# Attention on one Trainium2 core: weighing the values for two key chunks at a time

## The chip, the cores and the metric

The kernel runs on one core of one Trainium2 chip. The metric is the device time of one execution in microseconds (us). A core has the engines PE (TensorE, matmul; its weight loads are listed as PEld), DVE (VectorE), ACT (ScalarE), POOL (GpSimd) and the DMA queue of SP (SyncE). They run side by side and wait for each other through semaphores.

## The reference

The program is one transformer layer: a modulated layer norm, causal attention, and a routed feed-forward part. Only the attention is touched by the change. Its core, for 8 sequences of 1024 tokens, 16 heads of 32 columns:

```python
q, k, v = proj(w_q, b_q), proj(w_k, b_k), proj(w_v, b_v)          # 8 x 16 x 1024 x 32 each
scores = jnp.einsum('bhqd,bhkd->bhqk', q, k) / np.sqrt(D_K)
scores = jnp.where(causal, scores, -jnp.inf)
attn = jax.nn.softmax(scores, axis=-1)
out = jnp.einsum('bhqk,bhkd->bqhd', attn, v).reshape(B, S, D_MODEL)
```

## The kernel before, in words

The program has five stages: modulation, the projections to q, k and v, attention, output projection with routing and shared part, and the experts. Attention works on 32 groups (8 sequences times 4 groups of 4 heads), one after the other, as a pipeline over groups: while the probabilities of one group (`prev` in the code) are computed, the row maxima of the next group (`cur`) are found.

The probabilities of a group are cut into 12 chunks. A chunk is one block of 128 keys against one half (512) of the queries, for all four heads; the list `chunks` gives (half, key block) of each. Because attention is causal, a chunk has 512, 384, 256 or 128 columns. In this text a *place* c is the part of a group's step in which chunk c is computed (chunks count from 0), c = 0 to 11. At a place PE issues, for each of the four heads h:

- one matmul that gives the scaled scores of chunk c minus the row maximum (L871, tile `ps_p`, three banks), and a masking matmul where the chunk lies on the diagonal (L874). ACT makes exponentials of it (L718) in a tile `pt`. The matmul waits until the exponential three matmuls earlier is done, since it takes over its bank;
- `TILES[4c+h]` score tiles of the next group (function `scores`, L815, tile `ps_s`, four banks). DVE takes the row maxima of each (L751, L757). A score tile waits until the maxima four tiles earlier are done. There are 48 score tiles in a group, spread over places 0 to 9.

After the four heads of place c, PE *weighs* the chunk before, c-1: `weigh` (L825) multiplies exponentials by values and adds up in the bank `ps_o`. Each head gives only 32 output rows, so four such matmuls stand beside each other in the array (128*32 in the profile, "column-tiled"); a chunk takes 8 instructions in the trace. The chunks 10 and 11 of a group are weighed at place 11 and at place 0 of the next group.

The sums of the exponentials are made in two steps. POOL *joins* tiles of exponentials (`join`, L677: one tile added into another in place, as `INTO` says), which works when the chunk was weighed, and PE multiplies what is left by ones (`total`, L842, column-tiled as well): one tile for the first query half at place 8, two tiles for the second half, of the group before, at place 3 (`TOTAL_AT`). A total takes one of the four `ps_s` banks, at the position that `BEFORE` works out from `TOTAL_AT`; ACT copies it out (L703) and the bank is free again.

At place 10 (`TURN`) PE transposes the row maxima (L850), DVE negates them and splits them in a high and a low part (L769, L771), and SP writes both as two more rows of the queries in SBUF (L628). The first matmul of place 0 of the next group waits for them (`m_in`). The order of everything is written out by hand; there is no scheduler.

Of the kernel before, what the change touches and what calls it, by code (L numbers as in the profile page):

```python
# [20 lines left out]
GH = P // HD  # L21
# [19 lines left out]
CREDIT = 16  # L41
# [414 lines left out]
def stage_attention(nc, qk_dram, v_dram, o_dram, inv_dram):  # L456
# [14 lines left out]
    with ExitStack() as ctx:  # L471
# [49 lines left out]
        NPROB = NC * GH  # L521


        INTO = {1: 0, 2: 0, 3: 0, 5: 4, 7: 6, 8: 4, 9: 4, 10: 6, 11: 6}
        JOINS = sorted(INTO)
        NJ = len(JOINS)
        HEADS = [[0], [4, 6]]
        TOTAL_AT = (8, 3)
        LATER = (3, 11)


        TILES = [3, 0, 1, 1, 1, 2, 1, 1, 2, 1, 1, 0, 2, 1, 1, 1, 2, 0, 1, 1,
# [115 lines left out]
        def _(pool):  # L648
# [21 lines left out]
            def join(group, c):  # L670

                col = span(c)
                into = tile(INTO[c])[:, :, col:UNIT]
                pool.wait_ge(pv_done, CREDIT + NC * group.g + c + 1)
                pool.sem_inc(mark, 1)
                pool.wait_ge(add_done, CREDIT + NJ * group.g + JOINS.index(c))
                pool.tensor_tensor(into, into, tile(c)[:, :, col:UNIT], ALU.add).then_inc(add_done, 1)  # L677
# [11 lines left out]
        def _(act):  # L689
# [15 lines left out]
            def step(cur, prev):  # L705
                if not prev:
                    return
                for c in range(NC):
                    col = span(c)
                    user, back = user_before(c)  # L710
                    for h in range(GH):
                        n = c * GH + h
                        if h == 0 and user in INTO:
                            act.wait_ge(add_done, CREDIT + NJ * (prev.g - back) + JOINS.index(user) + 1)
                        if h == 0 and user not in INTO:
                            act.wait_ge(sum_done, CREDIT + QH * (prev.g - back) + chunks[user][0] + 1)
                        act.wait_ge(p_done, CREDIT + NPROB * prev.g + n + 1)
                        act.activation(tile(c)[:, h, col:UNIT], ps_p[n % NP][:, col:UNIT], ACT.Exp,  # L718
                                       scale=float(HD) ** -0.5).then_inc(exp_done, 1)
                        group = prev if c >= 2 else older(prev)  # L720
                        if h == 0 and (c - 2) % NC in ENDS and group:
                            take(group, (c - 2) % NC)
                        if h == 0 and c == TOTAL_AT[0] + 1:
                            take_total(prev, 0)
                        if h == 0 and c == TOTAL_AT[1] + 1 and older(prev):
                            take_total(older(prev), 1)
# [70 lines left out]
        def _(pe):  # L797
# [20 lines left out]
            def weigh(group, c):  # L818
                qh, kt = chunks[c]
                col = span(c)  # L820
                if kt == 0:
                    pe.wait_ge(o_free, CREDIT + QH * group.g + qh)
                pe.wait_ge(exp_done, CREDIT + NPROB * group.g + (c + 1) * GH)
                for h in range(GH):
                    last = pe.matmul(ps_o[h * HD:(h + 1) * HD, col:UNIT], vs[group.slot][:, kt, h * HD:(h + 1) * HD],  # L825
                                     tile(c)[:, h, col:UNIT], start=kt == 0, stop=c in ENDS)
                last.then_inc(pv_done, 1)
# [24 lines left out]
            def step(cur, prev):  # L852
# [6 lines left out]
                for c, (qh, kt) in enumerate(chunks):  # L859
# [17 lines left out]
                            scores(cur, prev, share[n], share[n + 1])  # L877
                    group = prev if c else older(prev)
                    if group:
                        weigh(group, (c - 1) % NC)  # L880
                    if c == TOTAL_AT[0]:
                        total(prev, 0, cur)
                    if c == TOTAL_AT[1] and older(prev):
# [1 line left out]

            steps(step)(pe)
            end = Group(GROUPS - 1, (GROUPS - 1) % SLOT, None)
            weigh(end, NC - 1)
            total(end, 1, None, alone=(NC - 2, NC - 1))

# [941 lines left out]
```

## Time and profile before

| what | value |
|---|---|
| median of 3 runs | 3338.03 us (3325.95 to 3339.06) |
| the profiled execution | 3321.04 us, its span 3319.3 us |
| attention | from 695 to 1870 us of the span, 31 turns of about 36.7 us and the two ends |
| PE in a group of 36.70 us | 36.33 us busy |
| DVE, ACT, POOL in the same group | 26.19, 22.63, 27.99 us busy |

A line of the timeline has the start in us from the start of the span, the time, the engine, the line of the kernel, the operation, the tiles written and read, the shape, and how many instructions were merged. In square brackets stands how long the engine was idle before it and what released it. The time of a matmul is modelled and overlaps with the next; how long a piece of work really takes on PE is therefore read from start to start. Idle time on PEld in front of a column-tiled load is put down to whatever semaphore that instruction also waits for, even where that had been given long before.

### The profile page before, as it was taken

To read this page: it belongs to the slowest core of one execution; us is meant where nothing else is said; L and a number is where in the kernel's file an instruction comes from. 1 tells how busy PE (TensorE), PEld (TensorE's weight loads), DVE (VectorE), ACT (ScalarE), POOL (GpSimd) and SP (SyncE) were. 2 spreads that over 40 slices of the span, in tenths; PEclk is the share of its full clock that TensorE was granted. 3 is DMA by queue.
4 is the path that set the end of the run, shared out by engine and by line. 5 is a ranking of instruction groups with operands and counts; after the bars stand their busy time and mean duration, and the time that the engine had idled before them with its cause. 6 is when DMAs were issued, how large, how long until landed. Compare 5 with 4: busy or idle time off the path is not lost. (4 is left out here: it accounts for less than half of the span.)

```text
span 3319.3 us, 52119 instructions
## 1 busy us (share of the span) xinstructions
PE 3023.0 (91%) x16704; PEld 2188.1 (66%) x16704; DVE 2144.3 (65%) x5331; ACT 1384.5 (42%) x2755; POOL 1888.6 (57%) x1107
## 2 busy tenths in 40 slices
PE   3999999789999999999999669999999999966997
PEld 0888888655556556555656258777777777745776
DVE  3545555377767776777677257778777777735674
ACT  1212222136666666566666432332332233214674
POOL 2332332237777777777777525565664765653664
PEclk7999999979999999999999789999999999977998
DMA  8556555555445544554453323323323223107996
GB/s 163 172 173 209 180 199 174 160 123 129 111 105 127 131 105 105 129 129 104 111 129 79 100 81 111 102 67 98 114 67 98 89 92 92 60 13 214 236 241 132
DMA packets 297669, 419.49 MB, mean 126 GB/s; under 512 B 64776, under 2 KB 148744, under 8 KB 297495
## 3 DMA queue, kind: packets, MB, share of 16 engines
q1 hardware_dynamic: 274974, 383.70, 41.9%
q0 software_dynamic: 22528, 33.72, 5.2%
q8 instruction: 86, 1.41, 0.2%
q14 instruction: 81, 0.66, 0.1%
HBM read 262.85 MB, written 153.01 MB: 125 GB/s over the span
## 5 line engine op out<-in xcount | busy, mean ns | idle before, releaser
L677 POOL TENSOR_TENSOR att_pt<-att_pt 128x2048 f32<-128x2048 f32 (+3 forms) x286 | 892.2, 3120 | 319.2 <-PE att_ps_o L825 306.0
L718 ACT ACTIVATE att_pt<-att_ps_p 128x512 f32<-128x512 f32 (+3 forms) x1536 | 679.7, 496 | 491.8 <-PE att_ps_p L874 291.9
L751 DVE CUSTOM_DVE_ANT_0 att_ps_s<-att_ps_s,att_causal 128x512 f32<-128x512 f32 (+3 forms) x1024 | 492.8, 505 | 152.4 <-PE att_ps_s L815 148.8
L871 PE MATMUL att_ps_p<-att_qs,att_ks 98*128 98x512 f32 (+3 forms) x1536 | 555.3, 386 | 6.7 <-DMA att_qs<-att_m_lo 3.2
L815 PE MATMUL att_ps_s<-att_ks,att_qs 96*128 96x512 f32 (+3 forms) x1536 | 487.9, 375 | 22.7 <-DMA att_ks<-qk_parts 22.0
L871 PEld LDWEIGHTS att_ps_p<-att_qs,att_ks 98*128 98x128 f32 x1536 | 288.9, 190 | 280.3 <-ACT att_pt L718 172.9
L757 DVE TENSOR_REDUCE att_lower<-att_ps_s 128x1 f32<-128x512 f32 x512 | 352.0, 688 | 178.7 <-PE att_ps_s L815 176.9
L1140 POOL DMA_INDIRECT slot_info<-ffn_info,ffn_slot x256 | 272.8, 1065 | 123.9 <-issue 77.6
L815 PEld LDWEIGHTS att_ps_s<-att_ks,att_qs 96*128 96x128 f32 x1536 | 278.1, 194 | 76.0 <-issue 22.4
L825 PE MATMUL att_ps_o<-att_pt,att_vs 128*32 128x512 f32 (+3 forms) x3072 | 328.0, 499 | 0.0
L311 POOL TENSOR_TENSOR qkv_x<-qkv_x,qkv_mod 128x512 f32<-128x512 f32 x64 | 91.1, 1424 | 363.6 <-DVE qkv_x L378 363.6
L1104 POOL TENSOR_TENSOR ffn_h<-ffn_h,ffn_mod 128x512 f32<-128x512 f32 x48 | 75.1, 1564 | 301.9 <-DVE ffn_h L1258 301.9
L874 PE MATMUL att_ps_p<-att_mask_k,att_ident_r 128*128 128x128 f32 x1024 | 240.1, 238 | 0.0
L1422 PE MATMUL ffn_ps_m<-ffn_dn_hi,ffn_a_hi 128*128 128x512 f32 x512 | 210.1, 410 | 9.1 <-DVE ffn_a_lo L1383 6.1
L400 DVE SCALAR_TENSOR_TENSOR qkv_out_lo<-qkv_ps_m,qkv_bqk,qkv_out_hi 128x512 fp32r<-128x512 f32 x128 | 93.4, 746 | 178.3 <-ACT qkv_out_hi L355 178.3
L1422 PE MATMUL ffn_ps_m<-ffn_dn_hi,ffn_a_lo 128*128 128x512 f32 x512 | 204.7, 400 | 2.4 <-issue 2.4
L1422 PE MATMUL ffn_ps_m<-ffn_dn_lo,ffn_a_hi 128*128 128x512 f32 x512 | 205.2, 401 | 1.3 <-issue 1.2
L1422 PE MATMUL ffn_ps_m<-ffn_hT_hi,ffn_up_hi 128*128 128x512 f32 x512 | 202.3, 395 | 3.3 <-issue 3.2
L1422 PE MATMUL ffn_ps_m<-ffn_hT_lo,ffn_up_hi 128*128 128x512 f32 x512 | 200.4, 391 | 3.6 <-issue 3.6
L1422 PE MATMUL ffn_ps_m<-ffn_hT_hi,ffn_up_lo 128*128 128x512 f32 x512 | 200.6, 392 | 2.7 <-issue 2.6
L443 PE MATMUL qkv_ps_m<-qkv_hT_hi,qkv_w_hi 128*128 128x512 f32 x512 | 200.5, 392 | 1.5 <-DVE qkv_hT_lo L383 1.5
L443 PE MATMUL qkv_ps_m<-qkv_hT_lo,qkv_w_hi 128*128 128x512 f32 x512 | 200.2, 391 | 0.0
(263 smaller groups left out, 6229.3 us busy)
## 6 DMA issues: line engine op xcount, KB each, us to landing
att_qs<-qk_parts SPq DMA_DIRECT2D x96, 512.0 KB, 6.8
att_ks<-qk_parts SPq DMA_DIRECT2D x96, 512.0 KB, 13.2
qk_parts<-qkv_out_hi SPq DMA_DIRECT2D x128, 256.0 KB, 2.6
qk_parts<-qkv_out_lo SPq DMA_DIRECT2D x128, 256.0 KB, 2.9
qkv_x<-x SPq DMA_DIRECT2D x16, 1024.0 KB, 5.5
v_rows<-qkv_out_v SPq DMA_DIRECT2D x64, 256.0 KB, 2.3
att_vs<-v_rows SPq DMA_DIRECT2D x32, 512.0 KB, 16.0
o_parts<-att_o SPq DMA_DIRECT2D x64, 256.0 KB, 6.6
```

The source lines that it names most:

```text
L400: dve.scalar_tensor_tensor(out_lo[n % RING][:, :], ps_m[n % BANKS][:, :], bqk_sb[:, n:n + 1], raw(out_hi[n % RING][:, :]), op0=ALU.add, op ...
L443: last = pe.matmul(ps_m[n % BANKS][:, :], w_part[:, k, (n % NG) * P:(n % NG + 1) * P], h_part[:, k, :], start=k == 0 and a + c == 0, stop= ...
L677: pool.tensor_tensor(into, into, tile(c)[:, :, col:UNIT], ALU.add).then_inc(add_done, 1)
L718: act.activation(tile(c)[:, h, col:UNIT], ps_p[n % NP][:, col:UNIT], ACT.Exp, scale=float(HD) ** -0.5).then_inc(exp_done, 1)
L751: dve.tensor_tensor_reduce(bank, bank, causal[:, UNIT - (c1 - c0):UNIT], scale=1.0, scalar=MASKED, op0=ALU.add, op1=ALU.max, accum_out=row ...
L757: dve.reduce_max(lower[:, low:low + 1], bank, axis=AX.X).then_inc(max_done, 1)
L815: pe.matmul(ps_s[at % NS][:, 0:c1 - c0], qs[cur.slot][0:STACK, h, t * P:(t + 1) * P], ks[cur.slot][0:STACK, h, c0:c1], start=True, stop=Tr ...
L825: last = pe.matmul(ps_o[h * HD:(h + 1) * HD, col:UNIT], vs[group.slot][:, kt, h * HD:(h + 1) * HD], tile(c)[:, h, col:UNIT], start=kt == 0 ...
L871: last = pe.matmul(ps_p[n % NP][:, col:UNIT], ks[prev.slot][:, h, kt * P:(kt + 1) * P], qs[prev.slot][:, h, q0:(qh + 1) * UNIT], start=Tru ...
L874: last = pe.matmul(ps_p[n % NP][:, col:col + P], ident_r[:, :], mask_k[:, :], start=False, stop=True)
L1140: pool.indirect_dma_start(info_dram[:, :], bass.IndirectOffsetOnAxis(slot[half][:, j:j + 1].bitcast(U32), 0), info[half][:, j, :], None, b ...
L1422: last = pe.matmul(bank, a[m], c[n], start=i + j == 0, stop=i + 1 == len(pairs) and j == 2)
```

## The change

Three things are changed. A table `RUNS` now says at which place which chunks are weighed: chunks 0 and 1 at place 2, 2 and 3 at place 4, 4 and 5 at place 6, 6 and 7 at place 8, chunk 8 at place 9, chunk 9 at place 10, and 10 and 11 together at place 0 of the next group. Places 1, 3, 5, 7 and 11 weigh nothing. The total of the second half moves from place 3 to place 2 (`TOTAL_AT`), where it stands right behind the weighing of chunk 1 and not of chunk 2, and the bank that it takes moves with it. A join now waits for the exponentials of the chunk that it reads and for the weighing of the tile that it writes, and no longer for the weighing of the chunk that it reads; that wait has gone to ACT, which now asks for it before it overwrites the tile. Chunk 7 is joined into the tile of chunk 4 instead of that of chunk 6, which is weighed only at place 8.

```diff
-        INTO = {1: 0, 2: 0, 3: 0, 5: 4, 7: 6, 8: 4, 9: 4, 10: 6, 11: 6}
+        INTO = {1: 0, 2: 0, 3: 0, 5: 4, 7: 4, 8: 4, 9: 4, 10: 6, 11: 6}
-        TOTAL_AT = (8, 3)
+        TOTAL_AT = (8, 2)
+        RUNS = {0: (10, 11), 2: (0, 1), 4: (2, 3), 6: (4, 5), 8: (6, 7), 9: (8,), 10: (9,)}
@@ join
-                pool.wait_ge(pv_done, CREDIT + NC * group.g + c + 1)
+                pool.wait_ge(exp_done, CREDIT + NPROB * group.g + (c + 1) * GH)
+                pool.sem_inc(mark, 1)
+                pool.wait_ge(pv_done, CREDIT + NC * group.g + INTO[c] + 1)
@@ scalar step
                             act.wait_ge(add_done, CREDIT + NJ * (prev.g - back) + JOINS.index(user) + 1)
+                            act.wait_ge(pv_done, CREDIT + NC * (prev.g - back) + user + 1)
@@ tensor step
                     group = prev if c else older(prev)
                     if group:
-                        weigh(group, (c - 1) % NC)
+                        for done in RUNS.get(c, ()):
+                            weigh(group, done)
@@ tensor, behind the last group
+            weigh(end, NC - 2)
             weigh(end, NC - 1)
```

The first place to look at is the end of one group and the start of the next, on PE. Before, from the last head of place 11 on; pt5 holds chunk 10 and pt6 chunk 11:

```order
L874 MATMUL att_ps_p2<-att_mask_k,att_ident_r 128x128
L825 MATMUL att_ps_o<-att_pt5,att_vs0 32x256 [waits att_exp]
L825 MATMUL att_ps_o<-att_pt5,att_vs0 32x256 x3
L871 MATMUL att_ps_p0<-att_qs1,att_ks1 128x512 [waits att_v_in1,att_exp,att_m_in1,att_q_in2]
```

In the changed kernel, from the same instruction to the end of place 0, on PE (lines are 4 higher there):

```order
L878 MATMUL att_ps_p2<-att_mask_k,att_ident_r 128x128
L875 MATMUL att_ps_p0<-att_qs1,att_ks1 128x512 [waits att_v_in1,att_exp,att_m_in1,att_q_in2]
L878 MATMUL att_ps_p0<-att_mask_k,att_ident_r 128x128
L819 MATMUL att_ps_s0<-att_ks2,att_qs2 128x512 [waits att_mlo]
...
L819 MATMUL att_ps_s0<-att_ks2,att_qs2 128x512 [waits att_max]
L829 MATMUL att_ps_o<-att_pt5,att_vs0 32x256 [waits att_exp]
L829 MATMUL att_ps_o<-att_pt5,att_vs0 32x256 x3
L829 MATMUL att_ps_o<-att_pt6,att_vs0 32x128 [waits att_exp]
L829 MATMUL att_ps_o<-att_pt6,att_vs0 32x128 x3
```

The weighing of chunk 10 has moved behind the work of place 0, to that of chunk 11; the matmul that waits for the rows of the maxima (`att_m_in1`) now follows place 11 directly.

The second is places 2 and 3, on PE, the weighings and the total alone. Before, pt0, pt3 and pt4 hold chunks 0, 1 and 2, pt1 and pt2 what is to be summed of the group before, and between the weighings stand the matmuls of a place each:

```order
L825 MATMUL att_ps_o<-att_pt0,att_vs1 32x512 [waits att_exp,att_o_free]
...
L825 MATMUL att_ps_o<-att_pt3,att_vs1 32x384 [waits att_exp]
...
L825 MATMUL att_ps_o<-att_pt4,att_vs1 32x256 [waits att_exp]
L825 MATMUL att_ps_o<-att_pt4,att_vs1 32x256 x3
L842 MATMUL att_ps_s3<-att_pt1,att_ones 32x512 [waits att_add,att_max]
L842 MATMUL att_ps_s3<-att_pt1,att_ones 32x512 x3
L842 MATMUL att_ps_s3<-att_pt2,att_ones 32x512 x4
```

In the changed kernel, the end of place 2 on PE:

```order
L829 MATMUL att_ps_o<-att_pt0,att_vs1 32x512 [waits att_exp,att_o_free]
L829 MATMUL att_ps_o<-att_pt0,att_vs1 32x512 x3
L829 MATMUL att_ps_o<-att_pt3,att_vs1 32x384 [waits att_exp]
L829 MATMUL att_ps_o<-att_pt3,att_vs1 32x384 x3
L846 MATMUL att_ps_s2<-att_pt1,att_ones 32x512 [waits att_add,att_max]
L846 MATMUL att_ps_s2<-att_pt1,att_ones 32x512 x3
L846 MATMUL att_ps_s2<-att_pt2,att_ones 32x512 x4
```

Chunk 0, chunk 1 and the total are now one stretch of column-tiled matmuls, in which no score tile is issued; chunk 2 has gone to the end of place 4, and the total takes bank 2 instead of bank 3.

## Rows read from the trace of the kernel before

**Rows 1.** Busy time by engine in one group, turn to turn; of each engine, busy us and instructions.

```profile
core 0: us, PE busy (x) PEld busy (x) DVE busy (x) ACT busy (x) POOL busy (x), PEclk, DMA share, GB/s
1208.80:1245.50 36.70, 36.33 (x249) 21.90 (x249) 26.19 (x85) 22.63 (x53) 27.99 (x10) 1.00 0.53 117
```

**Rows 2.** Timeline of PE, turn and end of place 11.

```profile
1208.84 0.27 PE L850 MATMUL att_ps_s<-att_ident,att_rowmax 128*32 128x128 f32 x1 [0.30 <-DVE att_rowmax L764]
...
1212.06 0.33 PE L871 MATMUL att_ps_p<-att_qs,att_ks 98*128 98x128 f32 x1
...
1212.43 0.64 PE L825 MATMUL att_ps_o<-att_pt,att_vs 128*32 128x256 f32 x8
1213.00 0.50 PE L871 MATMUL att_ps_p<-att_qs,att_ks 98*128 98x512 f32 x1
```

**Rows 3.** Timeline of PE, places 7 to 9 of that group.

```profile
1237.74 1.06 PE L825 MATMUL att_ps_o<-att_pt,att_vs 128*32 128x512 f32 x8
1238.73 0.50 PE L871 MATMUL att_ps_p<-att_qs,att_ks 98*128 98x512 f32 x1
1239.08 0.23 PE L815 MATMUL att_ps_s<-att_ks,att_qs 96*128 96x128 f32 x1
...
1239.66 0.40 PE L871 MATMUL att_ps_p<-att_qs,att_ks 98*128 98x512 f32 x1
1239.90 0.40 PE L815 MATMUL att_ps_s<-att_ks,att_qs 96*128 96x512 f32 x1
...
1240.37 0.51 PE L815 MATMUL att_ps_s<-att_ks,att_qs 96*128 96x128 f32 x2
1240.81 0.85 PE L825 MATMUL att_ps_o<-att_pt,att_vs 128*32 128x384 f32 x8
1241.48 1.04 PE L842 MATMUL att_ps_s<-att_pt,att_ones 128*32 128x512 f32 x8
```

**Rows 4.** Timeline of PE, end of place 2: a weighing of 384 columns alone.

```profile
1221.07 0.85 PE L825 MATMUL att_ps_o<-att_pt,att_vs 128*32 128x384 f32 x8
1221.86 0.33 PE L871 MATMUL att_ps_p<-att_qs,att_ks 98*128 98x128 f32 x1
```

**Rows 5.** Timeline of ACT, the exponentials of place 11.

```profile
1211.73 1.08 ACT L718 ACTIVATE att_pt<-att_ps_p 128x128 f32<-128x128 f32 x4 [1.04 <-PE att_ps_p L874]
```

**Rows 6.** Who waited for whom in attention (us in total, times, longest).

```profile
PEld att_ps_s L815 <- ACT att_total L703: 9.0, 30, 0.3
```

**Rows 7.** Timeline of POOL: joins.

```profile
1205.18 16.61 POOL L677 TENSOR_TENSOR att_pt<-att_pt 128x1536 f32<-128x1536 f32 x5 [1.61 <-PE att_ps_o L825]
```

**Rows 8.** Timeline of PE: the total at place 3.

```profile
1224.29 1.90 PE L842 MATMUL att_ps_s<-att_pt,att_ones 128*32 128x512 f32 x16
```

**Rows 9.** Timeline of DVE: idle behind the turn and the total; then three tiles.

```profile
1213.88 0.69 DVE L757 TENSOR_REDUCE att_lower<-att_ps_s 128x1 f32<-128x512 f32 x1 [3.93 <-PE att_ps_s L815]
...
1226.99 0.57 DVE L751 CUSTOM_DVE_ANT_0 att_ps_s<-att_ps_s,att_causal 128x384 f32<-128x384 f32 x1 [1.68 <-PE att_ps_s L815]
...
1229.74 0.69 DVE L757 TENSOR_REDUCE att_lower<-att_ps_s 128x1 f32<-128x512 f32 x1
...
1231.20 0.69 DVE L757 TENSOR_REDUCE att_lower<-att_ps_s 128x1 f32<-128x512 f32 x1
```

**Rows 10.** Timeline of PE: places 5 and 6, each with the weighing behind it.

```profile
1228.58 0.50 PE L871 MATMUL att_ps_p<-att_qs,att_ks 98*128 98x512 f32 x1
...
1230.80 1.07 PE L825 MATMUL att_ps_o<-att_pt,att_vs 128*32 128x512 f32 x8
1231.79 0.50 PE L871 MATMUL att_ps_p<-att_qs,att_ks 98*128 98x512 f32 x1
...
1234.41 1.06 PE L825 MATMUL att_ps_o<-att_pt,att_vs 128*32 128x512 f32 x8
```

**Rows 11.** Timeline of SP, the second row of the maxima.

```profile
1210.04 0.59 SPq L628 DMA_DIRECT2D att_qs<-att_m_lo  x1
```

**Rows 12.** The tile m_lo in attention: issue to landing.

```profile
DMA to landing us min/median/max: 2.1/2.1/3.0
```

## The prediction

> **What bounds the kernel now.** I read the busy time by engine over one group first, then the timelines of PE, ACT, DVE and POOL over the same group, and last the list of waits. In a group of 36.70 us PE is busy for 36.33, and no other engine for more than 27.99 [rows 1]. The clock column there is 1.00, so PE runs at its upper level throughout. PE's only idle time of note is 0.30 us at the turn [rows 2]. So attention lasts as long as PE's instruction stream, and what counts is how long each piece really holds PE, read from start to start.
>
> There the stream has a price that the busy figure hides: a column-tiled stretch costs more than its work. Three parts of it can be read.
> - In front: two score tiles start at 1240.37; one of 512 columns takes 0.24 (1239.66 to 1239.90), one of 128 a quarter, 0.06, so the weighing could start at 1240.67; it starts at 1240.81. That is 0.14 us [rows 3].
> - At its end: a weighing of 384 columns with a full-width matmul behind it takes 0.79 us [rows 4], with another column-tiled stretch behind it 0.67 us (1240.81 to 1241.48) [rows 3]. That is 0.12 us.
> - Behind: the first full-width matmul holds PE for 0.35 us (1238.73 to 1239.08), a later one of the same size for 0.24 [rows 3]. That is 0.11 us.
>
> Together 0.37 us for each weighing that stands alone. A group has twelve such stretches now (the totals stand behind weighings) and seven after the change.
>
> **The change part by part.**
>
> Chunks 0, 2, 4 and 6 join the next chunk's weighing (four stretches fewer): 4 x 0.37 = 1.48 us. The multiplications themselves stay. Nothing lies beside this time, since PE is the engine that is full; what takes it back is whoever is late next, below.
>
> Chunk 10 goes from place 11 to place 0. Before, place 0 starts at 1213.00 [rows 2]. Now its first matmul directly follows place 11, but must have the exponential three matmuls back, the second of place 11. Those four start at 1211.73 and take 1.08, so the second ends at 1212.27 [rows 5]; the handover is 0.06 (the first ends at 1212.00, and the matmul that waits for it starts at 1212.06 [rows 2]). So place 0 starts at 1212.33, 0.67 earlier, and without the 0.11 behind a tiled stretch: 0.78. The work comes back at the end of place 0: 256 columns, about 0.42 (from 512 alone, 0.99, to 384 alone, 0.79, it is 0.20 for each 128 [rows 3, 4]; from 0.67 for 384 inside a stretch it is 0.22). Net 0.36 us; one wait, on ACT, is all that this edit uncovers.
>
> The second total moves from place 3 to place 2. It stands behind a weighing before and after, so it changes no stretch. But the bank that it takes is now asked for by a tile late in place 3, where ACT has only exponentials of 128 columns in front of the copy; before, PE waited for the copy in 30 groups, 9.0 us [rows 6], 0.30 each. I count 0.25 back; the ends are 0 and 0.30.
>
> The joins wait for exponentials. POOL is not what PE waits for as long as the second total finds its joins done. Before: five joins from 1205.18 to 1221.79 [rows 7], the total at 1224.29 [rows 8], 2.5 us to spare. Counted from the start of place 0 (1213.00), the joins start at -7.8. Now the 1.61 us of idle in front of them goes [rows 7] (chunk 7 no longer waits to be weighed), the join in front of that can start one weighing earlier (1.0, the first half of a pair being enough), and the shorter group costs 1.5: -8.9, and with 16.6 of work they end at 7.7. The total comes at 8.9: place 3 began at 1221.86, which is 8.86 [rows 4], plus 0.42 for chunk 10 and less 0.37 for a stretch. 1.2 us to spare: cost 0. Were that gone, each us of lateness would be a us of PE at place 2. The wait moved to ACT costs nothing either: the tile that it writes at place 8 was weighed at place 2, and the latest such pair is chunk 9, weighed at place 10 and overwritten at place 2 of the next group. Behind a late ACT stands PE, which needs its banks.
>
> What is late next is DVE, and that is the one new cost. Today every place has a weighing behind it, in which DVE catches up. Now two places follow each other, and PE may be four tiles ahead at most. Places 5 and 6 are the worst, with 12 tiles in `TILES`. DVE needs 1.46 us for three (1229.74 to 1231.20 [rows 9]), 0.49 each, 5.84 for twelve. PE took 2.22 and 2.62 for the two places, up to each weighing [rows 10]; less the 0.14 and 0.11 that go, 4.59. When PE issues the twelfth tile, eight of the twelve and about one and a half left over must be done: 9.5 x 0.49 = 4.6, and some 0.4 from the first tile to DVE's start, 5.0. PE is held for about 0.45 us. Ends: 0, if DVE is level at the start, and 5.84 - 4.59 = 1.25, if DVE paces both places. The pairs 1 and 2 (9 tiles), 3 and 4 (9) and 7 and 8 (10) I put at 0.10 together.
>
> Sum for a group: 1.48 + 0.36 + 0.25 - 0.45 - 0.10 = 1.54 us. There are 31 turns: 47.7 us. The last group, where no score tiles stand between and PE often waits for ACT, I put at 1.3, a little less than a turn: 49 us.
>
> The profiled execution took 3321.0 us (span 3319.3), and 3321.0 - 49 is 3272. The three timed runs are 3326 to 3339; with the profiled one the mean is 3331. I set the gain against that: 3282 us.
>
> At one point the Trainium skill speaks against this. Rows 3 let a column-tiled matmul follow another nearly free: 384 columns take 0.67 for some 0.60 to 0.64 of work. The Trainium skill ("TensorE: Matmul & The Clock Gate", Part 3: Packing small matmuls — row/col tiling) says that a weight load overlaps with matmuls in flight only if it goes to other rows of the array; column tiles share all rows. By that rule each of the five joints in the pairs would show its loads again, and I would put them at the 0.14 that the front of a stretch costs, in place of 0.03: 0.55 us a group, 17 us in all, and 3299 us. The trace had this joint 0.67 us long, which speaks for the row.
>
> **The rivals.**
>
> Half the gain (3299 to 3310 us). The mechanism is right, but more is given back: DVE holds PE by 1.25 us instead of 0.45, which leaves 0.74 us x 31 = 23 us, 3308. Or the rows of the maxima come late: the second is issued at 1210.04 [rows 11] and lands after 2.1 us, 1212.14, only 0.19 before place 0 can now start; the longest took 3.0 [rows 12], which would be 0.7 us late, and for all groups 22 us. For it: margins shrink from 0.86 to 0.19 us. Against it: minimum and median are both 2.1. The rule above belongs here too.
>
> No gain (3315 to 3347, the change doesn't do what it says). The 0.37 us might not be a price of changing width but of the wait for exponentials in which each weighing stands, in which case fewer stretches leave it where it is. Against it: the last scores matmul in front of each weighing has already waited for a later exponential than the weighing needs, and the 0.11 behind the stretch has nothing to wait for.
>
> Slower (3353 us). DVE becomes the bound. It works 26.2 us of a group and is idle for 10.5 [rows 1]: 3.93 at the turn and 1.68 behind the total, the rest smaller [rows 9]. After the change the tiled stretches last about 3.5 us at place 2 (0.99 + 0.67 + 1.9 [rows 3, 8]), 2.6 at place 8 and 1.9 at place 6. If DVE enters each with four tiles (1.95 us) it idles 2.0, 1.1 and 0.4 with the refill, and 3.8 around the turn, 7.3 in all: 33.5 us, below the 35.2 of PE. With two tiles only, as when PE's own waits keep it from running ahead, it loses 0.97 more at each of four stretches: 37.4 us a group, 0.7 over today, +22 us. It decides from 2.4 tiles down, (36.7 - 33.5) / 4 = 0.8 us less than four. Against it: today PE keeps DVE fed up to each weighing, and it will issue faster.
>
> **How the numbers follow.** What can be told from no change is about 0.5%, 17 us on 3331. Forecast 0.60, with its own range 3265 to 3298 (2.1 us a group with DVE never in the way; 1.05 with 0.95 of holding). Half the gain 0.24, no gain 0.10, slower 0.06. Faster by over 0.5%: 0.84; within: 0.10; slower: 0.06. For 8 in 10 I take 3260 to 3316, which holds the half gain and leaves out the last two cases.
>
> **What would show it.** Right: turns 35.1 to 35.3 us apart; a pair of 512 and 384 columns that takes about 1.65 us to the total; place 0 about 3.5 us behind the turn instead of 4.16; waits of PE for DVE's maxima, today hardly there, at places 5 and 6, with some 0.5 us a group; longer single idle times of DVE at place 3 (above 2 us) and none between 1 and 2; POOL idle before fewer joins. Wrong: a second chunk in a pair that takes 0.14 us more than its columns (the skill's rule); a wait for m_lo at every place 0; turns at 36 us with DVE without gaps (DVE the bound); or turns at 36.7 with idle time in front of the pairs (the price was a wait).

## The result

The changed kernel takes 3623.72 us (median of 4 runs, 3597.67 to 3641.42) against 3331.99 us before. The ratio is 1.0858, with a 95% interval of 1.0819 to 1.0898: about 290 us slower, where 49 us faster was forecast. Between the first and the last turn lie 31 turns: before, they take 36.79 us each on average (nearly all 36.70), now 46.04. 31 x 9.25 = 287 us, so attention holds the whole loss. In the experiments below, where some runs of a kernel lie more than 1.5% above its fastest (e5, e6, e10), the ratio is taken from the others and so is smaller than the quotient of the medians.

The page of the changed kernel, parts 1 and 2 (engine, busy us; below, slices of the span in tenths):

```profile
span 3633.0 us, 52405 instructions
...
PE 3248.5 (89%) x16704; PEld 2376.2 (65%) x16704; DVE 2213.6 (61%) x5331; ACT 1399.9 (39%) x2755; POOL 1886.7 (52%) x1107
...
PEclk7999999677788787877778777999999999997998
```

The last row is what to look at first. In the attention, where the old page has a 9 in every slice that lies wholly in it, the clock that was granted to TensorE is 7 or 8 tenths. No engine was given more work: the page of before has the same counts of instructions (16704 matmuls, 5331 on DVE, 1107 on POOL).

One group of the changed kernel, then the stretches before and behind its turn (columns as in [rows 1]; the clock stands behind the busy times):

```profile
core 0: us, PE busy (x) PEld busy (x) DVE busy (x) ACT busy (x) POOL busy (x), PEclk, DMA share, GB/s
1234.60:1237.30 2.70, 0.06 (x4) 0.00 (x0) 2.59 (x1) 0.45 (x1) 2.62 (x2) 1.00 0.00 0
1237.30:1242.60 5.30, 5.27 (x26) 3.48 (x26) 0.77 (x3) 2.14 (x7) 5.22 (x2) 0.55 0.04 8
1242.60:1252.80 10.20, 10.20 (x44) 7.95 (x45) 5.02 (x15) 4.94 (x11) 2.87 (x2) 0.50 0.27 69
```

PE stands still for 2.7 us with the clock still up; then the clock is at the lower of its two levels, 0.50, which is 1.2 GHz, through places 10 and 11 and well into the next group. DVE is busy through the idle time with a single instruction. The timelines of PE and DVE there:

```profile
1233.59 1.06 PE L829 MATMUL att_ps_o<-att_pt,att_vs 128*32 128x512 f32 x8
1237.33 0.27 PE L854 MATMUL att_ps_s<-att_ident,att_rowmax 128*32 128x128 f32 x1 [2.68 <-DVE att_rowmax L768]
```

```profile
1234.11 0.14 DVE L755 DVE_READ_ACCUMULATOR2_ANT att_rowmax<- 128x1 f32 x1
1234.40 2.79 DVE L768 TENSOR_TENSOR att_rowmax<-att_rowmax,att_lower 128x16 f32<-128x16 f32 x1
1237.64 0.28 DVE L773 TENSOR_SCALAR att_m_hi<-att_ps_s 32x128 fp32r<-32x128 f32 x1 [0.45 <-PE att_ps_s L854]
```

The idle time answers to the 0.30 us at the turn in [rows 2]. What made it is the last step of the row maxima, an elementwise maximum of 16 columns. It took 2.79 us. The same line over all groups (ns: least, median, longest), in the changed kernel and then before:

```profile
L768 DVE TENSOR_TENSOR att_rowmax<-att_rowmax,att_lower x32: 177/2786/2807, 687.1 to 2111.4; 128x16 f32<-128x16 f32 x32
```

```profile
L764 DVE TENSOR_TENSOR att_rowmax<-att_rowmax,att_lower x32: 175/415/420, 692.2 to 1832.5; 128x16 f32<-128x16 f32 x32
```

It needs 0.18 us. Even before it took 0.42 in 28 of 31 turns. The join tile around that time shows what it stood behind: the joins of POOL in flight from 1234 to 1238 in the changed kernel:

```profile
L680 POOL TENSOR_TENSOR att_pt<-att_pt x2: 4524/4530/4535, 1232.6 to 1237.2; 128x2048 f32<-128x2048 f32 x2
```

One join runs from 1232.6 for 4.53 us, to 1237.15; the next starts at 1237.2. DVE's instruction ends at 1237.19. Before, the join of 384 columns ran from 1205.18 to 1208.66 and DVE's instruction from 1208.28 to 1208.70: it stood behind the tail of a join then, too, for a quarter of a microsecond. The change moved the joins earlier ([rows 7]: five joins that began when chunk 7 was weighed), and so put a join of 512 columns over the turn.

So far this is read from two traces: a cause (DVE behind POOL), an idle time, a clock, and no proof that one makes the next.

### The profile page after: what moved, and what is told of

Its sections match the earlier page's. It is cut to its first block and busy times, and to the rows that moved or that the text cites. A ratio compares the mean times of both kernels' runs of the same rounds, so it can differ in the third digit from the quotient of the medians.

```text
span 3633.0 us, 52405 instructions
## 1 busy us (share of the span) xinstructions
PE 3248.5 (89%) x16704; PEld 2376.2 (65%) x16704; DVE 2213.6 (61%) x5331; ACT 1399.9 (39%) x2755; POOL 1886.7 (52%) x1107
## 5 line engine op out<-in xcount | busy, mean ns | idle before, releaser
L722 ACT ACTIVATE att_pt<-att_ps_p 128x512 f32<-128x512 f32 (+3 forms) x1536 | 694.2, 496 | 769.7 <-PE att_ps_p L878 635.4
L875 PE MATMUL att_ps_p<-att_qs,att_ks 98*128 98x512 f32 (+3 forms) x1536 | 641.4, 440 | 6.5 <-DMA att_qs<-att_m_lo 3.2
L819 PE MATMUL att_ps_s<-att_ks,att_qs 96*128 96x512 f32 (+3 forms) x1536 | 584.1, 435 | 23.3 <-DMA att_ks<-qk_parts 22.2
L875 PEld LDWEIGHTS att_ps_p<-att_qs,att_ks 98*128 98x128 f32 x1536 | 355.3, 233 | 198.1 <-issue 143.9
L819 PEld LDWEIGHTS att_ps_s<-att_ks,att_qs 96*128 96x128 f32 x1536 | 331.5, 228 | 99.8 <-issue 22.5
L829 PE MATMUL att_ps_o<-att_pt,att_vs 128*32 128x512 f32 (+3 forms) x3072 | 367.2, 598 | 0.0
L878 PE MATMUL att_ps_p<-att_mask_k,att_ident_r 128*128 128x128 f32 x1024 | 292.1, 286 | 0.0
L878 PEld LDWEIGHTS att_ps_p<-att_mask_k,att_ident_r 128*128 128x128 f32 x1024 | 266.4, 260 | 12.3
## 6 DMA issues: line engine op xcount, KB each, us to landing
att_ks<-qk_parts SPq DMA_DIRECT2D x96, 512.0 KB, 12.9
```

The lines of the kernel that those rows point to most:

```text
L819: pe.matmul(ps_s[at % NS][:, 0:c1 - c0], qs[cur.slot][0:STACK, h, t * P:(t + 1) * P], ks[cur.slot][0:STACK, h, c0:c1], start=True, stop=Tr ...
L875: last = pe.matmul(ps_p[n % NP][:, col:UNIT], ks[prev.slot][:, h, kt * P:(kt + 1) * P], qs[prev.slot][:, h, q0:(qh + 1) * UNIT], start=Tru ...
L878: last = pe.matmul(ps_p[n % NP][:, col:col + P], ident_r[:, :], mask_k[:, :], start=False, stop=True)
```

## Experiments

The theory: DVE's last maximum, with both inputs in SBUF, waits for the POOL instruction in flight; PE then idles at the turn; and this idle time brings the clock down for some 20 us of nearly every group. Rival A: the new order of the matmuls (nothing weighed at place 11, long column-tiled stretches) lowers the clock by itself. Rival B: DVE is late for lack of score tiles, and the wait only shows at this instruction.

The kernels of one series share a chip and the runs of the kernel before; these were 3327, 3244 and 3306 us for the three series, so ratios are what can be compared. "Turn" is the mean distance over 31 turns, from the first to the last, in the profiled execution; for e10 that was the longest of its runs (3582 us). "Clock" is the mean granted clock in attention, 1.00 being the upper level.

| kernel | ratio to before (95% interval) | turn, us | clock in attention |
|---|---|---|---|
| before | 1 | 36.79 | 1.00 |
| changed | 1.0858 (1.0819 to 1.0898) | 46.04 | 0.80 |
| e1 one input | 0.9936 (0.9913 to 0.9959) | 35.94 | 1.00 |
| e2 hold | 1.0009 (0.9985 to 1.0032) | 36.85 | 1.00 |
| e3 old joins | 1.0018 (0.9996 to 1.0040) | 36.74 | 1.00 |
| e4 fill | 1.0227 (1.0185 to 1.0269) | 38.67 | 1.00 |
| e5 before, DVE +2.4 | 1.0895 (1.0861 to 1.0929) | 46.28 | 0.85 |
| e6 before, DVE +1.2 | 1.0963 (1.0927 to 1.0999) | | |
| e7 joins alone | 1.0250 (1.0223 to 1.0278) | 39.61 | 0.95 |
| e8 before, one input | 0.9989 (0.9975 to 1.0003) | 36.62 | 1.00 |
| e9 e8 and DVE +1.2 | 1.0261 (1.0237 to 1.0285) | 39.38 | 0.95 |
| e10 e8 and DVE +2.4 | 1.0694 (1.0655 to 1.0733) | 45.77 | 0.82 |
| e11 e1 again | 0.9921 (0.9901 to 0.9941) | 35.95 | 1.00 |
| e12 e1, a tile moved | 0.9914 (0.9896 to 0.9933) | 36.07 | 1.00 |

### e1: the same maximum with one SBUF input

```diff
-        lower = s.sb("lower", [P, GH * LOW], FP32)
+        both = s.sb("both", [P, GH * LOW, 2], FP32)
@@ the two halves of a maximum go side by side into both
-                                                 accum_out=rowmax[:, h * KT + t:h * KT + t + 1]).then_inc(max_done, 1)
+                                                 accum_out=(both[:, h * LOW + t - LOW, 1:2] if t >= LOW else
+                                                            rowmax[:, h * KT + t:h * KT + t + 1])).then_inc(max_done, 1)
-                        dve.reduce_max(lower[:, low:low + 1], bank, axis=AX.X).then_inc(max_done, 1)
+                        dve.reduce_max(both[:, low, 0:1], bank, axis=AX.X).then_inc(max_done, 1)
@@ negate
-                dve.tensor_tensor(upper, upper, lower[:, :].rearrange("p (h t) -> p h t", t=LOW), ALU.max).then_inc(max_done, 1)
+                dve.reduce_max(upper, both[:, :, :].rearrange("p (h t) s -> p h t s", t=LOW), axis=AX.X).then_inc(max_done, 1)
```

> The changed kernel; only the last step of the row maxima on DVE is another instruction: the two halves of a maximum are written side by side in one tile and taken together by a reduction with one SBUF input, in place of a tensor_tensor with two. Theory (DVE's instruction with two SBUF inputs stands behind the POOL join in flight, PE idles 2.7 us at every turn, and its clock falls): the instruction takes about 0.2 us also while a join runs, the idle time of PE at the turn goes from 2.68 to 0.1 to 0.4 us, the granted clock of the attention stage from 0.80 to 0.99 or more, turns 35.1 to 35.3 us apart, 3275 to 3295 us. Rival A (the new order of the matmuls itself lowers the clock: nothing to weigh at place 11, longer column-tiled stretches): the idle time goes, but the clock stays near 0.8 and the time is 3520 to 3560 us. Rival B (DVE is behind for lack of tiles after the long stretches, and the wait only shows at that instruction): the wait moves to another line, over 3550 us.

Measured: 3306.47 us, ratio 0.9936, clock 1.00. From its timeline, all engines together around a turn:

```profile
1225.77 4.57 POOL L680 TENSOR_TENSOR att_pt<-att_pt 128x2048 f32<-128x2048 f32 x1
...
1226.75 1.06 PE L830 MATMUL att_ps_o<-att_pt,att_vs 128*32 128x512 f32 x8
...
1227.56 0.19 DVE L769 TENSOR_REDUCE att_rowmax<-att_both 128x16 f32<-128x32 f32 x1
...
1227.89 0.27 PE L855 MATMUL att_ps_s<-att_ident,att_rowmax 128*32 128x128 f32 x1
```

A join of 4.57 us is in the middle of its run, and DVE's step takes 0.19 us beside it. Nothing else was changed, and the joins are where the change put them. The 2.68 us are gone, the clock stays up, and what is left of the change is a small gain. Rivals A and B both asked for over 3500 us and fall. The operation was changed together with the number of its SBUF inputs, so this run alone doesn't say which of the two frees it. The time is 11 us above my range, the turns (35.94, for 35.1 to 35.3) 0.6 us above theirs; more on that below.

### e2: POOL holds one join until the turn is past

```diff
             def join(group, c):
 
+                if c == 8 and group.g + 1 < GROUPS:
+                    pool.wait_ge(max_done, CREDIT + NM * (group.g + 2))
+                    pool.sem_inc(mark, 1)
                 col = span(c)
```

> The changed kernel, and POOL does not start the join of chunk 8 before DVE's last maximum of the turn is done; instructions are the same, only that join starts later (about 2.2 us). Theory: the same instruction of DVE, now with no join in flight, takes 0.18 us instead of 2.79, the clock stays up, 3275 to 3300 us; POOL ends its joins 2.2 us later, which may cost a wait at the total of place 2 of up to 1 us a group (30 us at most). Rival A (the order of the matmuls lowers the clock): 3520 to 3560 us. Rival B: no change, about 3620.

Measured: 3333.60 us, ratio 1.0009, clock 1.00. The tensor_tensor with two inputs is back, and no join runs beside it; over all groups it takes

```profile
L771 DVE TENSOR_TENSOR att_rowmax<-att_rowmax,att_lower x32: 174/175/177, 687.9 to 1830.2; 128x16 f32<-128x16 f32 x32
```

So it is not the instruction alone but the join beside it. That no gain was left has its main reason in the waits of PE in attention (us in total, times, longest):

```profile
PE att_ps_s L849 <- POOL att_pt L683: 22.7, 29, 0.9
```

The total at place 2 now waits 0.8 to 0.9 us for the last join in nearly every group, since the join of chunk 8 began 2.3 us later than in e1. That leaves 1.3 to 1.4 us as what the joins had to spare, against the 1.2 worked out in the prediction. The time is 34 us above my range of 3275 to 3300, which did not include the wait (put at 30 us at most).

### e3: the old rule for the joins

```diff
-                pool.wait_ge(exp_done, CREDIT + NPROB * group.g + (c + 1) * GH)
-                pool.sem_inc(mark, 1)
-                pool.wait_ge(pv_done, CREDIT + NC * group.g + INTO[c] + 1)
+                pool.wait_ge(pv_done, CREDIT + NC * group.g + c + 1)
```

> The changed kernel with the rule for joins of before (a join waits until the chunk that it reads was weighed); pairs, total at place 2 and the tile that chunk 7 is joined into stay. Theory: chunk 7 is joined when it is weighed at place 8, as before, which puts the end of that join at DVE's last maximum as before (0.42 us), and the join of chunk 8 behind it; the clock stays up; turns 35.3 to 36 us (the last join may reach the total of place 2 late), 3280 to 3310 us. Rival A: 3520 to 3620 us, since the order of the matmuls is that of the changed kernel. Rival B: the same.

Measured: 3333.98 us, ratio 1.0018, clock 1.00. Over all groups:

```profile
L766 DVE TENSOR_TENSOR att_rowmax<-att_rowmax,att_lower x32: 176/417/421, 689.4 to 1828.0; 128x16 f32<-128x16 f32 x32
```

The step takes 0.42 us as before the change, because the join of chunk 7 again starts when the chunk is weighed and ends at DVE's step. So the pairs alone do no harm; it takes the joins' rule. How much of the harm that rule does by itself, e7 shows. The time is 24 us above my range: the late joins cost PE 12.9 us in 29 waits at the total of place 2.

### e4: PE is kept busy while DVE is blocked

```diff
             def turn(cur, prev):
                 if prev:
+                    n = TURN * GH
+                    pe.wait_ge(exp_done, CREDIT + NPROB * prev.g + n - NP + 1)
+                    for _ in range(10):
+                        pe.matmul(ps_p[n % NP][:, :], ks[prev.slot][:, 0, 0:P], qs[prev.slot][:, 0, 0:UNIT], start=True, stop=True)
```

> The changed kernel with ten more matmuls of full width (512 columns, 2.4 us at the upper clock) on PE just before the turn, into a bank that the next scores overwrite; DVE's instruction still stands behind the join. This parts idle time from clock: if the clock falls because PE stands idle, it now stays at 0.99 though the turn comes as late as before, and the time is 3331 - 48 + 31 x 2.5 = 3360 us (3345 to 3380). If the clock falls by anything else in the new order, it stays near 0.8 and the time is 3600 us or more.

Measured: 3408.66 us, ratio 1.0227. The timeline of PE around a turn, and of DVE; below, attention as a whole:

```profile
1266.59 1.06 PE L829 MATMUL att_ps_o<-att_pt,att_vs 128*32 128x512 f32 x8
1267.58 2.60 PE L855 MATMUL att_ps_p<-att_qs,att_ks 98*128 98x512 f32 x10
1270.40 0.27 PE L858 MATMUL att_ps_s<-att_ident,att_rowmax 128*32 128x128 f32 x1 [0.22 <-DVE att_rowmax L768]
```

```profile
1267.41 2.85 DVE L768 TENSOR_TENSOR att_rowmax<-att_rowmax,att_lower 128x16 f32<-128x16 f32 x1
```

```profile
720.00:1880.00 1160.00, 1146.32 (x7799) 734.59 (x7801) 845.40 (x2563) 677.52 (x1567) 845.12 (x272) 1.00 0.48 108
```

DVE is blocked for 2.85 us as in the changed kernel, the turn comes as late, but PE works through it, and the clock stays at 1.00. This is the run that parts the two costs. Against e1 the block costs 38.67 - 35.94 = 2.73 us a turn, 85 us in all. Against e4 the changed kernel, with the same block and PE idle in it, loses another 46.04 - 38.67 = 7.37 us a turn, 228 us: the clock. The time was 29 us above my range.

### e5 and e6: idle time in the old order, and a dose that was not one

```diff
                 dve.wait_ge(max_done, CREDIT + NM * cur.g + N1)
                 dve.sem_inc(mark, 1)
+                if prev:
+                    for k in range(4):
+                        dve.reduce_max(junk[:, k:k + 1], causal[:, :], axis=AX.X)
```

e6 has `range(2)`.

> The kernel before, with four useless reductions of 512 columns (0.60 us each, 2.4 us) on DVE in front of the last maximum of every turn: the order of the matmuls and the joins are those of before, only PE must idle at the turn as in the changed kernel. Theory (idle time of some 2.7 us at the turn is enough to lower the clock): the clock of attention falls to 0.8, turns 46 to 48 us apart, 3600 to 3660 us. Rival A (it takes the new order too, with nothing weighed at place 11): the clock stays at 1.00, turns 39.1 us, 3327 + 31 x 2.4 = 3400 us.

> The same with two reductions (1.2 us): a smaller idle time at the same place. If the clock depends on the length of the idle time: it stays up and the time is 3327 + 31 x 1.2 = 3364 us. If any wait of over 1 us there is enough: the clock falls in many groups and it is over 3500 us. I expect the first, without a number of the trace for where the limit lies.

Measured: 3535.72 us, ratio 1.0895, and 3561.28 us, ratio 1.0963 (the profiled execution of e6 took 3804 us, so that only its mechanism is read and no turn or clock stands in the table). The first ratio is as expected. The second is far from it: half the delay costs as much and a little more. The waits of PE (from 720 to 1840 us) and DVE's step in e6 say why:

```profile
PE att_ps_s L854 <- DVE att_rowmax L768: 102.6, 21, 4.9
```

```profile
L768 DVE TENSOR_TENSOR att_rowmax<-att_rowmax,att_lower x32: 174/3800/3805, 687.3 to 2358.0; 128x16 f32<-128x16 f32 x32
```

A delay of 1.2 us carried the step into the next join, the one of chunk 8, and there it stood for 3.8 us; with 2.4 us of delay it met the same join later and took 2.62, and PE idled for 4.9 us in both. The two kernels gave the same dose of idle time, so they show that the order of before loses its clock as well, but not how much idle time it takes. They also show how near the old kernel lay: 1.2 us later, and it is 9.6% slower. In e5 every turn has the same 4.89 us of idle time, and yet after the first few the distance from one to the next alternates between 42.7 and 49.4 us, and the stretches at the lower clock between 6.8 and 20.5 us: how long it stays down is not set by the idle time alone.

### e7: the rule for the joins alone

```diff
-        INTO = {1: 0, 2: 0, 3: 0, 5: 4, 7: 6, 8: 4, 9: 4, 10: 6, 11: 6}
+        INTO = {1: 0, 2: 0, 3: 0, 5: 4, 7: 4, 8: 4, 9: 4, 10: 6, 11: 6}
-                pool.wait_ge(pv_done, CREDIT + NC * group.g + c + 1)
+                pool.wait_ge(exp_done, CREDIT + NPROB * group.g + (c + 1) * GH)
+                pool.sem_inc(mark, 1)
+                pool.wait_ge(pv_done, CREDIT + NC * group.g + INTO[c] + 1)
@@ scalar step
+                            act.wait_ge(pv_done, CREDIT + NC * (prev.g - back) + user + 1)
```

> The kernel before with the new rule for joins alone (exponentials of the chunk read, weighing of the tile written, chunk 7 into the tile of chunk 4); weighings stay single, the total at place 3. Theory: the join of chunk 8 now starts about 1241.5 in the old trace's time, when its exponentials are done, and takes 4.6 us; DVE's last maximum, at 1245.0, stands behind it for about 1.1 us. PE idles some 1.2 us at the turn: 3327 + 31 x 1.0 = 3358 us if the clock stays, over 3500 us if it falls. Rival B (the stall needs the pairs): 3327 us, no change.

Measured: 3324.06 us against 3243.96, ratio 1.0250. DVE's step over all groups, then attention:

```profile
L767 DVE TENSOR_TENSOR att_rowmax<-att_rowmax,att_lower x32: 176/1482/1770, 688.0 to 1914.4; 128x16 f32<-128x16 f32 x32
```

```profile
720.00:1900.00 1180.00, 1135.47 (x7423) 682.76 (x7419) 814.11 (x2528) 680.21 (x1550) 834.73 (x269) 0.95 0.48 106
```

The step stands behind the join for 1.3 us, near the 1.1 expected. Most turns are 37.80 us apart, 1.1 above before; five of the 31 are between 45 and 50 us, those in which the clock fell. The expectation of 1.0 us a turn if the clock stays was right for 26 of them; it gave two cases, and what came lies between.

This also corrects what e3 alone would suggest. The joins' rule without the pairs costs 39.61 - 36.79 = 2.82 us a turn, the whole change 9.25. One turn of e7, POOL (the first of these joins is that of chunk 8), then DVE:

```profile
1201.64 13.03 POOL L679 TENSOR_TENSOR att_pt<-att_pt 128x2048 f32<-128x2048 f32 x4
```

```profile
1204.75 1.50 DVE L767 TENSOR_TENSOR att_rowmax<-att_rowmax,att_lower 128x16 f32<-128x16 f32 x1
```

DVE reaches its step 3.11 us after the join's start here and 1.78 us after it in the changed kernel (1234.40 against the join that begins at 1232.6). With the pairs the same join blocks 1.3 us longer, PE idles 2.68 us and not 1.37, and the clock falls at every turn and not at five.

### e8: the kernel before with one input

The edit is that of e1, on the kernel before.

> The kernel before with the reduction with one SBUF input in place of the last tensor_tensor of the maxima. Theory: even before, that instruction stood behind a join for 0.24 us (0.42 instead of 0.18 us, ending 0.04 us behind the join in nearly every group); 0.2 us x 31 = 6 to 8 us less, 3320 us. It also says how much of the gain of the changed kernel with the same edit is due to the pairs.

Measured: 3241.37 us against 3243.96, ratio 0.9989 with an interval to 1.0003: what the whole time can tell is no change, but the turns are 36.62 instead of 36.79 us apart (5 us in all), and the step takes 0.19 us. The change without that step, from e8 to e11 with the same maximum (on two chips, both at clock 1.00 in attention), is worth 36.62 - 35.95 = 0.67 us a turn on average, and in most turns 0.8.

### e9 and e10: the dose without the port

The two edits together: e8, and two or four useless reductions in front of the last step.

> The kernel before with the reduction with one SBUF input and two useless reductions on DVE (1.2 us) in front of it: the dose without the port. The runs with two and with four reductions both idled for 4.9 us at most, because the delayed tensor_tensor then stood behind the next join; here it can't. Theory: PE idles 1.2 us less the slack of 0.2 at the turn; if it is a matter of length, the clock stays up in most groups as in the joins-alone run (1.5 us there, 27 of 31 turns at full clock), turns 37.5 us, ratio 1.008 to 1.012. Rival A has nothing against this number: with the old order it expects no fall at any length.

> The same with four reductions (2.4 us), about the idle time of the changed kernel (2.68), in the old order of matmuls. Theory (idle time alone lowers the clock): the clock falls once in nearly every group, turns 45 to 48 us, ratio 1.08 to 1.10. Rival A (the new order is needed too): clock 1.00, turns 38.7 us, ratio 1.02.

Measured: 3392.77 and 3563.37 us against 3306.05, ratios 1.0261 and 1.0694. The step itself takes 0.18 us in every group of both now. (The expectation of e9 tells e7 a little wrong: PE idled for 1.37 us there, and 26 turns kept their clock, not 27.) The waits of PE and the clock in e9, then in e10:

```profile
PE att_ps_s L855 <- DVE att_rowmax L769: 37.4, 29, 1.6
```

```profile
720.00:1900.00 1180.00, 1139.12 (x7466) 685.35 (x7462) 816.79 (x2608) 684.41 (x1560) 838.47 (x271) 0.95 0.48 106
```

```profile
PE att_ps_s L855 <- DVE att_rowmax L769: 62.4, 25, 2.8
```

```profile
720.00:2100.00 1380.00, 1303.94 (x7484) 785.63 (x7487) 864.59 (x2677) 699.49 (x1564) 838.36 (x271) 0.82 0.41 91
```

In the old order of matmuls, with no join involved, idle time of 1.26 us (in 28 of the 31 turns; 1.61 at most) cost the clock in 4 of 31 groups, idle time of 2.45 us (in 26 turns; 2.80 at most) in 22 of them (turns over 45 us). So idle time at the turn is enough, and the longer it is the more often the clock falls: 4 of 31 at 1.26 us, 5 at 1.37 (e7), 22 at 2.45, all at 4.89 (e5). What picks the groups that lose it at one and the same length, no run shows. The ratio of e9 is 1.026 and not the 1.010 I had written: the four falls, of 12 us each, are 49 us that I had named in words and left out of the number. e10 is a little below its range (1.08 to 1.10), since nine groups kept their clock. Runs of e10 differ by 58 us; that the number of falls differs between them is likely, but only one was profiled. The changed kernel, with 2.7 us in all groups, lost its clock in every one. Whether the new order adds something between the 22 and the 31 was not tried: no run has 2.7 us of idle time in all groups without the pairs.

### e11 and e12: e1 again, and one tile moved

e11 is the kernel of e1 on another chip. e12:

```diff
-        TILES = [3, 0, 1, 1, 1, 2, 1, 1, 2, 1, 1, 0, 2, 1, 1, 1, 2, 0, 1, 1,
-                 2, 2, 1, 1, 1, 3, 0, 2, 3, 0, 0, 2, 1, 1, 1, 2, 1, 2, 0, 0] + 2 * GH * [0]
+        TILES = [3, 0, 1, 1, 1, 2, 1, 1, 2, 1, 1, 0, 2, 1, 1, 1, 2, 1, 1, 1,
+                 2, 2, 1, 1, 1, 2, 0, 2, 3, 0, 0, 2, 1, 1, 1, 2, 1, 2, 0, 0] + 2 * GH * [0]
```

> The changed kernel with the one-input reduction once more, beside a kernel before on this chip: ratio 0.991 to 0.995 if the gain of 1.00 us a turn (35.70 instead of 36.70) is all that counts: 31 us of 3244 to 3327.

> The same with one score tile moved from place 6 to place 4, so that the two places 5 and 6 hold 11 tiles instead of 12. If DVE's lag holds PE there (the one new cost of the pairs that was forecast, 0.45 us), turns get 0.1 to 0.3 us shorter than 35.70, 3 to 9 us in all; if not, no change.

Measured: 3277.38 us, ratio 0.9921 (0.9901 to 0.9941), and 3276.57 us, ratio 0.9914 (0.9896 to 0.9933). e1 holds on a second chip, clear of no change. e12 equals it, and the 0.1 to 0.3 us a turn that it was to gain did not come: from place 6 to place 7 it is 0.38 us quicker (4.40 instead of 4.78), from place 4 to 5 it is 0.48 slower (3.07 instead of 2.59), and the turns are 0.1 us further apart. The tile that was taken from one pair of places holds PE in the other. By the ratios both are below the kernel before, by 26 and 28 us, and so well below the changed one.

## Why the prediction was wrong, point by point

**The step that failed** is "The joins wait for exponentials", with its cost of 0. I looked at POOL only as the one who must deliver sums in time, and that part was right (1.2 us to spare worked out, 1.3 to 1.4 shown by e2). I moved five joins against everything else on the chip without asking who runs beside them. The trace of before had the warning in it: the step of 16 columns at the turn took 0.42 us in 28 of 31 turns and 0.18 to 0.23 in the other three, and the long ones ended 0.04 us behind a join. I read the row in [rows 2] that waits for it, 0.30 us, and took it as a fixed wait.

The Trainium skill has this rule ("SBUF — State Buffer", Who interferes with whom): a VectorE instruction with two SBUF inputs contends with a GpSimd instruction that reads SBUF, over an interface that they share, and the second to issue is fully blocked until the first finishes. The traces agree in each point: blocked to within 0.04 us of the join's end (2.79 us for 0.18), free with one input beside a join of 4.57 us (e1), free with two inputs and no join (e2). That it is the number of SBUF inputs and not the operation rests on what the Trainium skill says there, since e1 changed both.

The joins' rule alone blocks DVE for 1.3 us (e7); that the pairs move the turn closer to the join's start, and so make it 2.6, is a second thing that the prediction did not ask about.

**The rivals.** None of them named it. The slower one had DVE as the bound, for lack of tiles, at 3353 us; the place (DVE, at the turn) was near, the mechanism and the size were not. A point of the prediction's own list, "turns at 36 us with DVE without gaps", did not occur. With the step repaired, the gain is that of the first rival, half of what was forecast: about 0.8 us a turn in e11 for its 0.74, though by e11's waits for DVE only in part for its reason (below).

**What was left out** is that idle time of PE can cost more than itself. The clock column was read as 1.00 and taken as fixed. Of the 287 us in attention, 228 are the clock, 85 the block itself, and 26 come off for the rest of the change and e1's step together (e4, e1).

**What held.** With the step repaired, the times at place 2 are those that were worked out. Counted from the start of place 0, the second total comes at 8.9 us in e11 (8.9 forecast), and the joins that it needs run from -9.2 to 7.4 (-8.9 to 7.7 forecast). PE's first matmul of places 2, 4 and 8, now with no weighing before it, holds PE for 0.11 us less than in e8, as forecast; that of place 6 does not (0.34 us in both). At the joint of a pair, chunk 6 and 7 together with a total behind them take

```profile
1223.25 1.71 PE L830 MATMUL att_ps_o<-att_pt,att_vs 128*32 128x512 f32 x16
1224.78 0.61 PE L847 MATMUL att_ps_s<-att_pt,att_ones 128*32 128x512 f32 x4
```

1.53 us from start to start, for 0.99 + 0.67 = 1.66 apart [rows 3]. The 0.99 holds the 0.12 us at the end of a stretch, which the forecast of about 1.65 should have taken off; without it they are 1.54. So the weight loads of the second chunk cost nothing at the joint, and the rule of the Trainium skill that was set against the rows there does not describe these tiles. Place 0 starts 3.5 us behind the turn, as forecast, with no wait for the rows of the maxima. In the changed kernel itself much of this was hidden, because in most groups its places 10, 11 and 0 to 2 ran at the lower clock.

**What was mis-sized.** With the step repaired the change is worth 0.8 us in most turns, not 1.54. From e8 to e11, by stretches of places: 10, 11 and 0 together give 0.27 (forecast 0.36); places 1 to 4 give 0.61, where two stretches and the bank of the total made 0.99 less a part of 0.10; places 5 and 6 lose 0.18, where 0.37 was to be gained and 0.45 lost; places 7 and 8 give 0.14 of 0.37. Apart from chunk 10, 1.16 us of the forecast's gains are missing, where 0.55 was given to DVE's lag. The 0.45 us for places 5 and 6 was right within 0.1 us. PE's weight loads for score tiles waited for DVE, from 720 to 1800 us of e11 and then of e8 (us in total, times, longest):

```profile
PEld att_ps_s L820 <- DVE att_both L755: 11.7, 61, 0.3
PEld att_ps_s L820 <- DVE att_both L762: 7.6, 31, 0.3
PEld att_ps_s L820 <- DVE att_rowmax L755: 5.0, 31, 0.2
```

```profile
PEld att_ps_s L816 <- DVE att_both L758: 7.1, 29, 0.3
```

That is 24.3 for 7.1 us, or 0.57 us a group more, and the new waits stand at places 4, 6 and 8: DVE holds PE in the pairs with 9 and 10 tiles too, which had been put at 0.10 together. For the pair of places 1 and 2 they show next to nothing. e12 agrees: a tile less at one pair and one more at another moves the hold with it. So DVE's lag is seen for about half of the 1.16 us; to what the rest is due, a hold that these waits miss or a stretch that costs less than 0.37 us, stays open.

**A size that was only seen.** The stage behind attention varies: from its first to its last matmul it took 1071 us in the profiled execution of before, 1086 in the changed kernel and 1050 in e11, with code that was not changed. The clock is at its lower level for 88, 107 and 77 us of it in these three. What sets that was not studied; it is one reason why the whole time of e1 tells less than its turns.

## What to carry to other kernels

When a change moves work on an engine that is not the bound, ask not only who waits for its results but which instructions of its neighbours will now run beside it. Small steps on the path (16 columns, 0.18 us) deserve the look most; one that takes longer than its size asks for, and that always ends with another engine's instruction, is likely to stand behind that instruction, and will do so wherever it goes. Read the granted clock of every stage after a change before reading anything else: a fall of it turns a wait of 2.7 us into 10.

## What the runs showed of the hardware

- A DVE tensor_tensor of 128x16 with both inputs in SBUF took 0.18 us with no POOL instruction beside it (e2). Beside a POOL tensor_tensor of 128x2048 in flight it ended 0.03 to 0.04 us behind that one, after 1.48, 2.79 and 3.80 us in e7, the changed kernel and e6. A tensor_reduce over the same numbers with one SBUF input took 0.19 us beside a join in flight (e1).
- TensorE's clock fell from its upper to its lower level behind idle time at the turn: at 1.26 us of it in 4 of 31 groups (e9), at 1.37 us in 5 (e7), at 2.45 us in 22 (e10), at 2.68 us in every group of the changed kernel, at 4.89 us in every group of e5, and in none where matmuls filled 2.6 us of the same wait (e4). In the group shown it then stayed down from place 10 through most of place 2 of the next group (0.55 and 0.50 in the stretches above), though PE was busy throughout.
- Two column-tiled weighings in one bank, one behind the other, took 1.53 us (e11), the 1.66 us of the two read apart less the 0.12 us that the first of them loses at the end of a stretch when a full-width matmul follows.
